# First attention: values of two heads projected with the context stationary

## The reference

```
def _L0_xattn_ref(hidden_states, key_value_states, attention_mask, position_bias, ln_weight, w_q, w_k, w_v, w_out):
    x = _rmsnorm(hidden_states, ln_weight)
    h_q = (x @ w_q.T).reshape(b, lq, H, DH)
    h_k = (key_value_states @ w_k.T).reshape(b, lk, H, DH)
    h_v = (key_value_states @ w_v.T).reshape(b, lk, H, DH)
    score = jnp.einsum('bqhd,bkhd->bhqk', h_q, h_k) + position_bias[None]
    score = softmax(where(attention_mask, score, -inf))
    attn = jnp.einsum('bhqk,bkhd->bqhd', score, h_v).reshape(b, lq, H * DH)
    return hidden_states + attn @ w_out.T
```

## Time and profile before

| | us |
|---|---|
| median of 3 runs | 3171.32 (3167.78 to 3174.17) |
| the profiled execution | 3167.63 |
| its span | 3165.5 |
| TensorE busy | 2974.8 (94%) |
| VectorE busy | 1805.4 (57%) |
| ScalarE busy | 1050.0 (33%) |
| GpSimd busy | 1002.0 (32%) |
| mean granted clock | 0.982 |

### The profile page before, as it was taken

One profiled execution on the slowest core, in us unless ns is written; L12 is line 12 of the kernel. 1 busy time (PEld: TensorE's weight loads), 2 busy tenths in 40 slices (PEclk: granted clock), 3 DMA queues, 4 the chain that ended last, 5 costly groups with the idle time before them and its releaser, 6 DMA issues.

```text
span 3165.5 us, 46948 instructions
## 1 busy us (share of the span) xinstructions
PE 2974.8 (94%) x15712; PEld 2487.9 (79%) x15712; DVE 1805.4 (57%) x3657; ACT 1050.0 (33%) x3498; POOL 1002.0 (32%) x842
## 2 busy tenths in 40 slices
PE   4989999999998997989989999999989999999899
PEld 3778888888887875768877888888867888888687
DVE  7454444444454238878766666666674554454744
ACT  2322222222222215732234444444313333333332
POOL 3423334333322126533422222223213333332221
PEclk9999999999999999989999999999999999999999
DMA  3111111111111101101111100111011111110111
GB/s 103 43 34 38 42 42 42 42 42 42 35 43 47 40 20 41 33 25 37 44 31 31 32 25 26 33 33 33 24 34 37 34 36 40 39 33 20 44 45 45
DMA packets 69140, 119.71 MB, mean 38 GB/s; under 512 B 8746, under 2 KB 14250, under 8 KB 68642
## 3 DMA queue, kind: packets, MB, share of 16 engines
q1 hardware_dynamic: 69026, 118.26, 12.6%
HBM read 116.06 MB, written 2.10 MB: 37 GB/s over the span
## 4 chain that ended last, share of the span: by engine, by line
PE 83%; DVE 11%; ACT 3%; issue 2%; DMA 0%; DVEq 0%; ACTq 0%; SPq 0%
PE proj L382 38%; PE outp L382 22%; PE heado L873 6%; PE score L844 4%; PE turn L864 2%; PE score L382 2%; PE turn L796 1%; DVE stats L431 1%; PE outp L1741 1%; PE score L1326 1%; DVE x L1116 1%; DVE xnT L505 1%; ACT sq L956 1%; ACT tbuf L968 1%; ACT acts L987 1%
## 5 line engine op out<-in xcount | busy, mean ns | idle before, releaser
L382 PE MATMUL outp<-w_out,acts 128*128 128x512 f32 x3288 | 852.1, 404 | 20.0 <-DVE x L1116 11.4
L382 PE MATMUL proj<-xnT,w_in 128*128 128x512 f32 x3288 | 781.3, 394 | 6.5 <-DVE xnT L505 2.7
L382 PEld LDWEIGHTS proj<-xnT,w_in 128*128 128x128 f32 x3288 | 613.9, 189 | 136.4 <-issue 6.0
L382 PEld LDWEIGHTS outp<-w_out,acts 128*128 128x128 f32 x3288 | 600.4, 190 | 146.8 <-DVE x L1116 16.2
L382 PE MATMUL proj<-ctxT,w_kv 128*128 128x512 f32 x2304 | 554.3, 398 | 21.3 <-ACT big L920 15.0
L382 PEld LDWEIGHTS proj<-ctxT,w_kv 128*128 128x128 f32 x2304 | 432.3, 190 | 125.1 <-ACT big L920 23.7
L645 POOL TENSOR_TENSOR w_out<-ring,consts 128x512 fp32r<-128x512 f32 x96 | 105.2, 1096 | 928.0 <-PE outp L382 928.0
L1116 DVE TENSOR_TENSOR x<-x,outp 128x512 f32<-128x512 f32 x384 | 262.3, 685 | 190.3 <-PE outp L382 188.5
L923 DVE COPY big<-proj 128x512 f32<-128x512 f32 x136 | 93.9, 691 | 386.7 <-PE proj L382 386.6
L645 POOL TENSOR_TENSOR w_kv<-ring,consts 128x512 fp32r<-128x512 f32 x96 | 101.1, 1053 | 427.1 <-DMA ring<-in_L_wk 425.7
L1140 DVE TENSOR_TENSOR acts<-heado,acts 128x512 fp32r<-128x512 f32 x192 | 132.9, 692 | 174.1 <-ACT acts L987 174.1
(11 more groups left out here) (246 smaller groups left out, 3952.3 us busy)
## 6 DMA issues: line engine op xcount, KB each, us to landing
ring<-in_L_wq SPq DMA_DIRECT2D x96, 256.0 KB, 2.7
ring<-in_L_wo SPq DMA_DIRECT2D x96, 256.0 KB, 2.7
ring<-in_F_in SPq DMA_DIRECT2D x52, 256.0 KB, 2.7
ring<-in_L_wk SPq DMA_DIRECT2D x48, 256.0 KB, 2.7
ring<-in_L_wv SPq DMA_DIRECT2D x48, 256.0 KB, 3.8
ring<-in_F_out SPq DMA_DIRECT2D x41, 256.0 KB, 2.6
x<-in_x SPq DMA_DIRECT2D x2, 1024.0 KB, 7.0
ring<-in_ctxT SPq DMA_DIRECT2D x8, 256.0 KB, 4.6
```

Source lines behind the costliest of these rows:

```text
L382: mm = pe.matmul(bank_ap, w_ap(a, c), rhs(b, c), start=first and c == 0 and n == 0, stop=last and c == chunks - 1 and n == len(PASSES) - 1)
```

## The change

1. **Values, two heads at once.** In an even step TensorE projects the values of this head and the next (`project_values`). The context is stationary (128 tokens of it) and the value weights of two heads move, 256 columns: four fills of a bank, each of 2 token blocks x 12 matmuls, alternating between the two banks. The result has the keys' tokens on the partitions. `take_values_fill` copies each fill to `v_pair`, which lies where `vT` and `v` lay: ScalarE fills 0 and 2, VectorE fills 1 and 3.
2. **No turning.** `turn_values` and `take_values` are no longer called in this attention; the context matmuls read `v_pair`, and in an even step wait for both banks' copies.
3. **Place.** In even steps values stand between keys and queries; odd steps have keys and queries only. The first pair is projected at the start of the stage, where before head 0's values stood.
4. **Tiles.** A value tile holds half of the input channels of two heads' weights, laid out on the host before the launch; the count and size of the tiles stay. Both tiles of a pair stand side by side in the order.

```
+    OWN_FIRST = [("k", 0, 0), ("v", 0, 0), ("v", 0, 1), ("q", 0, 0), ("k", 0, 1), ("q", 0, 1)]
+    OWN_TILES = [("k", 0, 2), ("q", 0, 2), ("o", 0, 0), ("k", 0, 3), ("q", 0, 3), ("o", 0, 1), ("v", 0, 2), ("v", 0, 3),
+                 ("k", 1, 0), ("q", 1, 0), ("o", 0, 2), ("k", 1, 1), ("q", 1, 1), ("v", 1, 0), ("v", 1, 1), ("o", 0, 3)]
...
+        v_pair = big[:, 2:4, :].rearrange("p a n -> p (a n)").rearrange("p (b h d) -> p b h d", b=B, h=2)
...
             def split_kv(g, j, what):
+                if A.own_kv and what == "v":
+                    if not (isinstance(g, int) and g == 0 and j < 2):
+                        m.wait(pool, ("pfull", 1), A.projection(*((g, 0) if j >= 2 else (g - 1, 2)), "v") + 2)
+                    split(g, j, "v", (w_kv, w_kv2)[j % 2], 1)
+                    return
...
             if A.own_kv:
-                value = [] if is_last_group(g) and j == GH - 1 else [(*h1, "v")]
-                return value + ([] if over else [(*h2, "k"), (*h2, "q")])
+                value = [] if j % 2 or isinstance(g, int) and g == 0 and j == 0 else [(g, j, "v")]
+                return value if over else [(*h2, "k"), *value, (*h2, "q")]
...
+        def project_values(pe, A, g, j):
+
+            m = A.events
+            n = A.projection(g, j, "v")
+            m.wait(pe, "split", A.tile(g, j + 1, "v") + 1)
+            for fill in range(4):
+                half = fill % 2
+                m.wait(pe, ("pfree", half), n + fill // 2)
+                for k in range(2):
+                    t = slice((2 * fill + k) * S, (2 * fill + k + 1) * S)
+                    mm = pe_matmuls(pe, proj[half][:, k * 2 * P:(k + 1) * 2 * P], lambda a, c: ctxT[:, a, c, t],
+                                    lambda b, c: (w_kv, w_kv2)[c // 2][:, 1, b, c % 2 * 2 * P:(c % 2 + 1) * 2 * P])
+                mm.then_inc(m["pfull", half], 1)
...
+                    if A.own_kv and j % 2 == 0 and half == 0:
+                        for i in range(2):
+                            m.wait(pe, ("pfree", i), A.projection(g, j, "v") + 2)
...
+        def take_values_fill(engine, on_act, A, g, j, fill):
+
+            m = A.events
+            half = fill % 2
+            m.wait(engine, ("pfull", half), A.projection(g, j, "v") + 1 + fill // 2)
+            dst = big[:, 2 + fill // 2, fill % 2 * HALF:(fill % 2 + 1) * HALF]
+            copy_projection(engine, on_act, dst, proj[half][:, :], None).then_inc(m["pfree", half], 1)
```

More of the change, by code:

```diff
@@ L98, in __init__ @@
         self.projections = 2 * kv + GH
-        self.turns = 16 if self.own_kv else 12 if self.normed else 10
-        self.turns_first = 4 if self.normed else 2
+        self.turns = 8 if self.own_kv else 12 if self.normed else 10
+        self.turns_first = 0 if self.own_kv else 4 if self.normed else 2
         units, heads = 2 * NH, NH
-        turns = self.turns_first + self.turns * NG - (4 if self.normed else 2)
+        turns = self.turns_first + self.turns * NG - (0 if self.own_kv else 4 if self.normed else 2)
         calls = heads + NG if self.normed else 0
@@ L123, in new_kv @@
         return self.own_kv or j == 0
-    OWN_FIRST = [("k", 0, 0), ("v", 0, 0), ("q", 0, 0), ("k", 0, 1), ("q", 0, 1)]
-    OWN_TILES = [("v", 0, 1), ("k", 0, 2), ("q", 0, 2), ("o", 0, 0), ("v", 0, 2), ("k", 0, 3), ("q", 0, 3), ("o", 0, 1),
-                 ("v", 0, 3), ("k", 1, 0), ("q", 1, 0), ("o", 0, 2), ("v", 1, 0), ("k", 1, 1), ("q", 1, 1), ("o", 0, 3)]
+    OWN_FIRST = [("k", 0, 0), ("v", 0, 0), ("v", 0, 1), ("q", 0, 0), ("k", 0, 1), ("q", 0, 1)]
+    OWN_TILES = [("k", 0, 2), ("q", 0, 2), ("o", 0, 0), ("k", 0, 3), ("q", 0, 3), ("o", 0, 1), ("v", 0, 2), ("v", 0, 3),
+                 ("k", 1, 0), ("q", 1, 0), ("o", 0, 2), ("k", 1, 1), ("q", 1, 1), ("v", 1, 0), ("v", 1, 1), ("o", 0, 3)]
     SHARED_FIRST = [("k", 0, 0), ("v", 0, 0), ("q", 0, 0), ("q", 0, 1)]
@@ L162, in projection @@
         if self.own_kv:
-            if start and j == 0:
-                return "kvq".index(what)
-            return self.projections * g + (3 * j + "kqv".index(what))
+            if start and (j == 0 or j == 1 and what != "v"):
+                return {"k": (0, 4), "v": (1,), "q": (3, 5)}[what][j]
+            if start and (j, what) == (2, "k"):
+                return 6
+            if what == "v" and j >= 2 and isinstance(g, int) and g == NG - 1:
+                return self.projections * g + 10
+            return self.projections * g + {"k": (-2, 2, 4, 8), "q": (1, 3, 7, 9), "v": (5, 5, 11, 11)}[what][j]
         if start and j < 2 and what != "k":
@@ L174, in turn @@
         if self.own_kv:
-            order = ["T0", "T1", "V0", "V1"]
-            at = 4 * j
+            order = ["T0", "T1"]
+            at = 2 * j
         elif self.normed:
@@ L741, in new_values @@
         def new_values(A, g, j):
-            return A.new_kv((j + 1) % GH) and not (isinstance(g, int) and g == NG - 1 and j == GH - 1)
+            return not A.own_kv and A.new_kv((j + 1) % GH) and not (isinstance(g, int) and g == NG - 1 and j == GH - 1)
         def pending(A, g, j):
@@ L767, in project_head @@
             n = A.projection(g, j, what)
+            if A.own_kv and what == "v":
+                project_values(pe, A, g, j)
+                return
             w, slot, act = {"k": (w_kv, 0, ctxT), "v": (w_kv, 1, ctxT), "q": (w_in, j % 2, xnT)}[what]
-            if A.own_kv and what != "q" and j % 2:
+            if A.own_kv and what == "k" and j % 2:
                 w = w_kv2
@@ L872, in step @@
                     for b in range(BH):
-                        mm = pe.matmul(heado[:, b * P:(b + 1) * P], v[:, (half * BH + b) * S:(half * BH + b + 1) * S],
+                        n = half * BH + b
+                        mm = pe.matmul(heado[:, b * P:(b + 1) * P], v_pair[:, n, j % 2, :] if A.own_kv else v[:, n * S:(n + 1) * S],
                                        ptbuf[:, half, b * P:(b + 1) * P], start=True, stop=True)
@@ L901, in attention_pe @@
                 turn_for_sums(0, 0, "q", taken=(0, 0, "q"))
-            for half in range(2):
+            for half in range(2 if not A.own_kv else 0):
                 turn_values(-1, 3, half)
@@ L929, in take_projection @@
             half = 0 if on_act else 1
+            if A.own_kv and what == "v":
+                for fill in (half, half + 2):
+                    take_values_fill(engine, on_act, A, g, j, fill)
+                return
             m.wait(engine, ("pfull", half), A.projection(g, j, what) + 1)
@@ L1002, in attention_act @@
                 sum_squares(0, 0, "q")
-            take_values(act, True, A, -1, 3)
+            if not A.own_kv:
+                take_values(act, True, A, -1, 3)
             exps(0, 0, 0)
@@ L1169, in attention_dve @@
                 rms(0, 0, "q")
-            take_values(dve, False, A, -1, 3)
+            if not A.own_kv:
+                take_values(dve, False, A, -1, 3)
             for half in range(2):
@@ L2275, in layout @@
     a["vecs"] = vecs
-    a["L0_wq"], a["L0_wk"], a["L0_wv"] = (tiles(i[f"L0_xattn_w_{n}"]) for n in "qkv")
+    a["L0_wq"], a["L0_wk"] = (tiles(i[f"L0_xattn_w_{n}"]) for n in "qk")
+    a["L0_wv"] = i["L0_xattn_w_v"].reshape(NH // 2, 2 * P, 2, 2, P).transpose(0, 2, 4, 3, 1).reshape(NH, P, D)
     a["L0_wo"] = i["L0_xattn_w_out"].T.reshape(NH, P, D)
```

## The result

The changed kernel takes 3184.97 us (median of 4 runs, 3181.67 to 3192.01) against 3170.83 us for the kernel before: ratio (changed kernel's time over that of the kernel before) 1.0046, 95% interval 1.0028 to 1.0064. It is slower by 14 us where I forecast 21 us faster, and it lies outside my range. The profiled execution has a span of 3179.9 us, 14.4 more than before.

A forecast was written before the change was run, and what follows sets the result against it. TensorE, busy throughout the first attention's body, was taken as the bound. Removing transposes (-25.9 us), the new value projection (+4.4) and moved values (+0.8) sum to -20.7: 3146.9, plus 3.7 for a median, 3150.6 us; range 3138 to 3166.

The forecast's parts named there:

- edit 1, gross: First attention: removing the values' transposes on TensorE, with one wait for VectorE's copy, takes away 31.9 us.
- edit 1, handed to waits: First attention: longer waits for ScalarE's copy take back 3.8 us in 14 even steps and 2.2 us in the first two.
- edits 2 and 3: First attention: value projection with context stationary, 256 columns a matmul, costs 4.4 us; moving values into even steps 0.8 us.
- Both rivals on unhidden loads: Value matmuls: weight loads half hidden, 150 ns each, 3198 us, chance 0.08; or not hidden, 227 ns, 3317 us, chance 0.02.
- Not all of that arrives: Even steps: TensorE arrives 0.87 us earlier, the chain releasing it only 0.60, so 0.27 us each goes to a longer wait.
- the handed-over wait grows: Even steps of the first attention: 14 steps each lose a copy's 0.7 us more, 3160 us; chance 0.12.
- the removal of work: First attention: one row of transposes less, and 96 value matmuls in about 11.4 us.
- the place where the wait would show: Even step of the first attention: TensorE's wait for ScalarE at about 0.5 us.
- the queues of weights: GpSimd's splits and SyncE's tile loads: moving the value tiles costs nothing; a late key would show as a projection's wait.
- the wide bounds for a value matmul: 256-column value matmuls: from 112 ns (-6.4 us) to 128 ns (+18.2 us), with 119 ns taken.

The follow-up runs named there:

- act_first: Changed kernel plus 16 idle VectorE instructions, ScalarE copying the keys' first half ahead of the exponentials in the first attention: 3142.2 us, ratio 0.9912.
- the padded kernel: Changed kernel plus 16 idle instructions on VectorE, so later code stands where it stood before the change: 3173.2 us, ratio 1.0006.
- late_o: Changed kernel plus 16 idle VectorE instructions, output-weight splits put behind the next gated keys and queries: 3155.3 us, ratio 0.9933.
- no_turns: Kernel before, only the value transposes and their copies removed (context from untransposed values), plus 16 idle VectorE instructions: 3173.5 us, ratio 1.0009.
- pad8: Changed kernel plus 8 idle instructions on VectorE, its second-attention loop at place 1727: one run, 3198.0 us.
- before_act_first: Kernel before, only ScalarE's copy of the first projection put ahead of the exponentials: 3162.8 us, ratio 0.9976.
- before_shift: Kernel before plus 240 idle VectorE instructions ahead of the second attention's loop, which then starts at place 1975: 3191.5 us, ratio 1.0062.
- no_turns_act: Kernel before without value transposes and their copies, ScalarE's first copy ahead of the exponentials, 16 idle VectorE instructions: 3133.7 us, ratio 0.9879.

## Why the prediction was wrong, step by step

| step | forecast | measured, first attention unless said |
|---|---|---|
| edit 1, gross | -31.9 | -26.1 with the copy first |
| edit 1, handed to waits | +6.0 | +21.0 in the changed kernel (what -26.1 and +2.6 leave of -2.5); +29.2 in edit 1 alone (from -26.1 to +3.1) |
| edits 2 and 3 | +5.2 | +2.6 |
| first attention, sum | -20.7 | -2.5 |
| second attention | not in the sum | +16.8 |

*The value matmuls were priced right.* I took 119 ns for 256 columns. In the chain of act_first 144 matmuls, 96 of 256 columns and 48 of 512, take 22.40 us; 48 at the 230 ns of the earlier trace rows are 11.0, which leaves 11.4 for 96: 118 to 119 ns. A load of its own, 112 ns in the earlier trace rows, hides beside each. Both rivals on unhidden loads, and the Trainium skill's sentence that I weighed against the rows, fall. The same section of that page of the Trainium skill also lets a load that targets the background weight buffer run ahead of matmuls in flight, which I had left out.

*The step that failed in the first attention* is the paragraph under edit 1 that begins "Not all of that arrives". It moved VectorE's chain up by the copy that leaves it and kept each of its durations, which gave 0.27 us a step for the longer wait. The listed waits are 1.3 us each instead (17.2 us in 13). The rows that it used were taken at the old distance between the last output product and the normalisation. Taking away the group of transposes that stood ahead of that product brings GpSimd's split, which the product releases, onto VectorE's operations. The earlier trace rows starts with VectorE at 418.99 and leaves out the split at 420.32 that stood in the same answer, with one slowed operation beside it (0.79 us for 0.16). The split would have been half a microsecond earlier, and four operations of the chain stood in its reach. My first rival, "the handed-over wait grows", has the right place and sign, but priced the wait at 0.7 us for another reason, the values' own copies; behind the first value fill the chain runs through all 120 projection matmuls without a wait (418.92, 17.19 us).

*The step that was missing* is an account of what edits do to the code that follows. "Nothing outside this stage is edited, so all that follows is a sum over its 32 heads" is false: the later stage's instructions did move. Neither fault turns the sign alone. With this one only, the forecast gain of 20.7 less 16.8 leaves about 4 us faster than before; with the first only it is the padded kernel, which measures the same as before. Together they make the change slower: -2.5 and +16.8 are +14.3, and the span grew by 14.4.

*Right* were the removal of work, the place where the wait would show, the queues of weights (no projection waits for a split) and, of the wide bounds for a value matmul, the centre. That centre was a choice between two bounds and not a derived number, so its nearness (119 for 118) is in part luck.

## What to carry to other kernels

Work taken from the engine that bounds a stage also moves every release that it gives: list what each of these starts on GpSimd and VectorE, and what it will run beside. A copy that frees a bank should stand ahead of longer work that it does not depend on. And when an edit changes the number of instructions ahead of a loop of more than 256, compare the later stages' times first; a few idle instructions are a cheap test.

## What the runs showed of the hardware

- A loop of 272 instructions on VectorE costs some 17 us in six passes at places 1719 and 1975 (3.2 to 3.7 us at each branch back), 27 at 1727 (724.5 us for 697.9), and nothing at 1735.
- A GpSimd product of two operands in SBUF and VectorE's do not run side by side in these rows: VectorE's 0.69 us becomes 1.47 to 1.49, its 0.16 becomes 1.04 or 1.05, and GpSimd's 1.29 becomes 1.63. The slowed 1.05 us operation ends at 413.32, with the split beside it at 413.31.
- A matmul of 256 columns with a weight load of its own takes 118 to 119 ns at full clock (122 in the changed kernel's chain of 17.19 us, right behind the wait), one of 512 columns 230.
- The stage behind the second attention is not steady. In the profile of the padded kernel its 136-column matmuls all run at half clock (granted clock 0.50 from 2309.7 to 2330.0); in the changed kernel's the granted clock is 0.92 over the group and 1.00 from 2332 on:

```profile
L387 PE MATMUL proj<-w_in,xnT x96: 415/415/462, 2309.7 to 2330.0; 128*128 128x136 f32 x96
```

That is 20.3 us against 11.6, and from the first of them to the end of the span it is 861.1 us against 850.6. Profiles of late_o, no_turns and pad8 have it too, those of before, after, act_first, before_act_first, before_shift and no_turns_act do not. It is a likely reason why the padded kernel's time falls 4 us short of what its second attention regains: 6 of its 12 runs have a mean granted clock of 0.977 or 0.978 and take 3173.8 to 3178.2 us, the others 0.979 or 0.980 and 3166.5 to 3172.6. How often this stretch is the cause in runs without a profile stays open.
